# Selective scan in three clipped adds a step, with one group's decay on GpSimd, y copies on ScalarE and B's tables loaded ready-made

## What is computed

```python
xr, gate = jnp.split(x @ W_in.T, 2, axis=-1)
xc = jax.nn.silu(conv4(xr + t_emb))                  # depthwise, 4 taps
xn = layer_norm(xc) * ln_g + ln_b
Bm, Cm, dt = jnp.split(xn @ W_xproj.T, 3, axis=-1)
Ad = 1.0 + jnp.tanh(dt @ W_dt.T + b_dt) * 0.01 * A
Bd = Bm * jnp.minimum(norm(xn), 1.0)

def step(h, inputs):                                 # 64 steps, one after the other
    ad, bd, xt, ct = inputs
    h = jnp.clip(h * ad[:, :, None] + bd[:, :, None] * xt[:, None, :], -10.0, 10.0)
    yt = jnp.einsum('bd,bdh->bh', ct, h)
    return (h, yt)
...
return (y + D * xn) * jax.nn.silu(gate) @ W_out.T
```

## Time and profile before

| | us |
|---|---|
| median of 3 runs | 1787.09 (1785.98 to 1788.56) |
| the profiled execution, its own time | 1789.41 |
| its span, first to last instruction | 1787.6 |
| layer 2, pass 0, three written-out blocks (24 steps) | 80.8 |
| layer 3, the same | 80.4 |
| layer 3, the other 104 steps of the scan | 264.4 |
| one rolled block of eight steps | 20.3 |

### The profile page before, as it was taken

One profiled execution on the slowest core, in us unless ns is written; L12 is line 12 of the kernel. 1 busy time (PEld: TensorE's weight loads), 2 busy tenths in 40 slices (PEclk: granted clock), 3 DMA queues, 4 the chain that ended last, 5 costly groups with the idle time before them and its releaser, 6 DMA issues. The chain is left out here.

```text
span 1787.6 us, 42368 instructions
## 1 busy us (share of the span) xinstructions
PE 1637.6 (92%) x13764; PEld 703.0 (39%) x13764; DVE 1613.1 (90%) x2452; ACT 1296.5 (73%) x2197; POOL 621.5 (35%) x576
## 2 busy tenths in 40 slices
PE   7999999999999999888888889999997888888898
PEld 3555555555554455322111114444452221111144
DVE  5899999999986999889999998679998899999985
ACT  5655556455546999889999993069998899999920
POOL 0223233232331221365655560002223566555500
PEclk9999999999999999799999999999997999999999
DMA  4000000000001335544555666724445545556668
GB/s 162 2 1 0 1 2 32 2 1 0 1 1 72 139 149 177 191 163 132 182 160 188 219 189 202 239 83 157 144 159 185 179 132 183 155 189 196 189 223 288
DMA packets 126445, 226.56 MB, mean 127 GB/s; under 512 B 35617, under 2 KB 61217, under 8 KB 117537
## 3 DMA queue, kind: packets, MB, share of 16 engines
q1 hardware_dynamic: 125904, 223.30, 38.1%
q10 hardware_dynamic: 432, 1.84, 0.3%
HBM read 141.73 MB, written 83.36 MB: 126 GB/s over the span
## 5 line engine op out<-in xcount | busy, mean ns | idle before, releaser
L1038 ACT ACTIVATE R<-q,Ast 128x512 f32<-128x512 f32 x1008 | 627.0, 709 | 20.3 <-DVE q L2018 15.3
L2018 DVE CUSTOM_DVE_ANT_0 q<-R,PS 128x512 f32<-128x512 f32 x1008 | 617.3, 771 | 15.9 <-ACT R L1038 14.4
L1479 PE MATMUL PS<-xq,Uw 96*128 96x512 bf16 x1024 | 350.0, 396 | 82.3 <-DVE q L2018 71.4
L613 POOL TENSOR_TENSOR Uw<-Ub,rowmask 96x512 bf16<-96x512 bf16 x256 | 335.5, 1346 | 252.1 <-PE PS L1479 252.1
L1492 PE MATMUL PS<-q,Wy 128*32 128x512 f32 x2048 | 284.5, 618 | 0.3
L1479 PEld LDWEIGHTS PS<-xq,Uw 96*128 96x128 bf16 x1024 | 85.6, 97 | 471.1 <-DVE q L2018 399.3
L1152 PE MATMUL PS<-X,Win 128*128 (+1 forms) x456 | 214.5, 607 | 0.1
L1053 PE MATMUL PS<-xn,Wl 128*128 128x512 f32 x384 | 186.5, 609 | 0.8 <-DVE xn L1605 0.7
L1723 DVE SCALAR_TENSOR_TENSOR acc<-xp,Wc,acc 128x512 f32<-128x512 f32 x192 | 134.7, 752 | 2.6
L547 POOL TENSOR_TENSOR ex<-ex,rs 128x1024 f32<-128x1024 f32 x32 | 76.8, 2400 | 164.2 <-DVE rs L1628 164.2
L1152 PEld LDWEIGHTS PS<-X,Win 128*128 128x128 f32 x456 | 82.5, 191 | 92.5 <-issue 91.7
(11 more groups left out here) (159 smaller groups left out, 2491.9 us busy)
## 6 DMA issues: line engine op xcount, KB each, us to landing
xq<-xpart_d SPq DMA_DIRECT2D x384, 192.0 KB
sg_d<-sg SPq DMA_DIRECT2D x16, 1024.0 KB, 5.1
xn_d<-z SPq DMA_DIRECT2D x16, 1024.0 KB, 3.9
y_d<-ys SPq DMA_DIRECT2D x64, 256.0 KB, 3.9
xnp<-xn_d SPq DMA_DIRECT2D x16, 1024.0 KB, 8.4
sgp<-sg_d SPq DMA_DIRECT2D x16, 1024.0 KB, 11.5
xpart_d<-xh SPq DMA_DIRECT2D x16, 512.0 KB, 2.9
xpart_d<-xmi SPq DMA_DIRECT2D x16, 512.0 KB, 3.8
```

The source lines that it names most:

```text
L613: pl.tensor_tensor(Uw[0:XROWS, h, w, :, :, :], Ub[0:XROWS, w, 0:N, ds(s0, CH)].rearrange("p n t -> p t n").unsqueeze(2).broadcast_to([XROW ...
L1038: act.activation(R[:, w, :], q[:, (t + 1) % 2, w, :], ACT.Copy, scale=Ast[:, h, w, t:t + 1]).then_inc(ac_r, 1)
L1479: pe.matmul(PS[:, w, :], Uw[0:XROWS, h, w, t, :, :].rearrange("p b n -> p (b n)"), xq[0:XROWS, hb, w, s8 % XT, :], start=True, stop=True). ...
L2018: v._custom_dve(bass.dve_ops.TENSOR_ADD_SAT, out=q[:, s8 % 2, w, :], in0=R[:, w, :], in1=PS[:, w, :], s0=CLIP, s1=-CLIP).then_inc(dv_q, 1)
```

## The change

- **Three adds a step.** DVE's `step` adds columns 0 to 767 (group 0 and half of group 1), 768 to 1535 (the other half and group 2) and 1536 to 2047 (group 3), in this order; I call them add 0, add 1 and add 2. The four PSUM banks and the four tiles of `R` and `q` lie side by side, so one instruction runs across them. Add 0 waits for the matmuls of groups 0 and 1, add 1 for that of group 2, add 2 for that of group 3.
- **Group 1's decay on POOL** (`half_decay`), in two halves of 256 columns, with the counter `pd_r` ("decayed_odd_ready"). ACT keeps groups 0, 2 and 3; `ac_r` is now called "decayed_even_ready".
- **y copies** (`keep_y`) go from DVE to ACT.
- **B's tables.** B is turned on PE in the front (`turn_b`), split on DVE from PSUM and stored by `store_b` in pieces of 16 values into `bdiag_d`, an array in HBM that was filled with zeros once. `load_x` then reads finished block-diagonal weights `Uw`, 72 rows, with one more DMA for two steps. POOL's `Uw` instructions, the tables `Ub`, their clearing, `rowmask` and the rows of ones go away; `xq` and `Uw` have 72 rows in place of 96.
- The conversion `xmi` of the last group goes from POOL to ACT, and its `xlo` is done in halves between POOL's decays.

```diff
-                    for w in range(QW):
-                        v.wait_ge(pe_w, pi * (QW * S) + n * QW + w + 1 + W0)
-                        if w % 2 == 0:
-                            v.wait_ge(pe_yq, pi * (2 * S) + n * 2 - 4 + w // 2 + 1 + USED)
+                    for p, (begin, end, groups) in enumerate(((0, SPLIT, 2), (SPLIT, 2 * SPLIT, 3), (2 * SPLIT, QW * DI, QW))):
+                        state = q[:, s8 % 2, :, :].rearrange("p w c -> p (w c)")[:, begin:end]
+                        fed = PS[:, 0:QW, :].rearrange("p w c -> p (w c)")[:, begin:end]
+                        v.wait_ge(pe_w, pi * (QW * S) + n * QW + groups + W0)
+                        if p < 2:
+                            v.wait_ge(pe_yq, pi * (2 * S) + n * 2 - 4 + p + 1 + USED)
...
-                        v.wait_ge(ac_r, pi * RS + n * QW - QW + w + 1 + READY)
+                        if p < 2:
+                            v.wait_ge(pd_r, pi * (2 * (S - 1)) + n * 2 - 2 + p + 1 + READY)
+                        v.wait_ge(ac_r, pi * (3 * (S - 1)) + n * 3 - 3 + p + 1 + READY)
                         alone(v)
-                        v._custom_dve(bass.dve_ops.TENSOR_ADD_SAT, out=q[:, s8 % 2, w, :], in0=R[:, w, :], in1=PS[:, w, :],
+                        v._custom_dve(bass.dve_ops.TENSOR_ADD_SAT, out=state, in0=R[:, :, :].rearrange("p w c -> p (w c)")[:, begin:end], in1=fed,
                                       s0=CLIP, s1=-CLIP).then_inc(dv_q, 1)
...
                     for w in range(QW):
-                        if t == 0:
-                            pe.wait_ge(pl_u, cn * QW + w + 1)
-                        pe.wait_ge(dv_q, pi * (QW * S) + n * QW + w + 1)
-                        pe.matmul(PS[:, w, :], Uw[0:XROWS, h, w, t, :, :].rearrange("p b n -> p (b n)"),
+                        pe.wait_ge(dv_q, pi * (UN * S) + n * UN + (1, 2, 2, 3)[w])
+                        pe.matmul(PS[:, w, :], Uw[0:XROWS, hb, s8 % XT, w, :, :].rearrange("p b n -> p (b n)"),
                                   xq[0:XROWS, hb, w, s8 % XT, :], start=True, stop=True).then_inc(pe_w, 1)
...
+                def half_decay(pi, c2, s8, p):
+                    h, t = s8 // CH, s8 % CH
+                    if t < 2 and p == 0:
+                        pl.wait_ge(pl_a, pi * CHUNKS + c2 * 2 + h + 1)
+                    pl.wait_ge(dv_q, pi * (UN * S) + c2 * (8 * UN) + UN * s8 + p + 1)
+                    alone(pl)
+                    cols = slice(p * (DI // 2), (p + 1) * (DI // 2))
+                    pl.tensor_tensor(R[:, 1, cols], q[:, (t + 1) % 2, 1, cols], Ast[:, h, 1, t:t + 1].broadcast_to([P, DI // 2]),
+                                     ALU.mult).then_inc(pd_r, 1)
...
-                            for w in range(QW):
-                                act.wait_ge(dv_q, cn * (QW * CH) + QW * t + w + 1)
+                            for p, w in enumerate((0, 2, 3)):
+                                act.wait_ge(dv_q, cn * (UN * CH) + UN * t + p + 1)
                                 act.activation(R[:, w, :], q[:, (t + 1) % 2, w, :], ACT.Copy,
                                                scale=Ast[:, h, w, t:t + 1]).then_inc(ac_r, 1)
+                            if t == 1 and h == 0 and before:
+                                keep_y(pi, c2 * 2 - 1, 1)
...
+                def turn_b(it, dst):
+                    pe.wait_ge(rB_r, it + 1)
+                    pe.transpose(dst, rB[:, :], ident[:, :]).then_inc(bt_mm, 1)
...
+                pe.wait_ge(tv_s, (l * G + G - 2) * 4 + 2 + TV0)
                 for m in range(DC):
                     variance(l * G + G - 1, m, 6)
...
                 def load_x(ps, k):
+                    rows = bdiag_d[ps, 0:GB * DIAG].rearrange("(r f) -> r f", f=S * ROW)
+                    sp.dma_start(Uw[0:XROWS, k % XB, :, :, :, :].rearrange("p t w b n -> p (t w b n)"),
+                                 rows[:, k * (XT * ROW):(k + 1) * (XT * ROW)].unsqueeze(0)
+                                 .broadcast_to([PARTS, GB * PARTS, XT * ROW])).then_inc(xq_in[k % XB], 16)
```

More of the change, by code:

```diff
@@ L184, in cond_resid_kernel @@
         late = ExitStack()
+        sb("table_gap", [P, TT * DI + P], where=late)
         pass_tables.append(tables(1, late))
@@ L316, in _ @@
             sp.dma_start(fold[:, :], fold_d).then_inc(ld_late, 16)
-            sp.dma_start(rowmask[:, :], rowmask_d).then_inc(ld_late, 16)
             sp.wait_ge(w_mm, G * 2)
+            sp.wait_ge(zero_r, 1)
+            for ps in range(PASSES):
+                rest = bdiag_d[ps, 0:GB * DIAG].rearrange("(p k c) -> p k c", p=P, c=1024)
+                for k in range(GB * DIAG // (P * 1024)):
+                    sp.dma_start(rest[:, k, :], words(zeros).bitcast(bf16)).then_inc(zero_in, 16)
             def load_front(n):
@@ new lines, in last_half, with last_group @@
+                def last_half(it, k, b):
+                    if b == 0:
+                        pl.wait_ge(xmi_r, it * TT + k + 1)
+                        alone(pl)
+                    cols = slice(b * (DI // 2), (b + 1) * (DI // 2))
+                    low = pl.tensor_tensor(xlo[:, k, cols], xr1[:, k, cols], xmi[:, k, cols], ALU.subtract)
+                    if b:
+                        low.then_inc(xlo_r, 1)
+                def last_group(n):
+                    it = l * G + G - 1
+                    if n == 20:
+                        pl.wait_ge(xq_st, it * 48 + 48)
+                        alone(pl)
+                    if 20 <= n < 20 + 2 * TT:
+                        last_half(it, (n - 20) // 2, n % 2)
@@ new lines, in eight @@
+                def eight(ps, c2, first=False, last=False, tail=False):
+                    pi = l * PASSES + ps
+                    for s8 in range(8):
+                        for p in range(2):
+                            if not (first and s8 == 0):
+                                half_decay(pi, c2, s8, p)
+                        if tail:
+                            last_group(c2 * 8 + s8)
+                        if s8 == 0:
+                            if not first:
+                                stage_decay(ps, c2, 1)
+                        elif s8 == 1:
+                            if not first:
+                                stage_outputs(ps, c2, 1)
+                        elif s8 == 4 and not last:
+                            stage_decay(ps, c2 + 1, 0)
+                        elif s8 == 5 and not last:
+                            stage_outputs(ps, c2 + 1, 0)
+                        elif s8 == 5 and ps + 1 < PASSES:
+                            pl.wait_ge(tab_in[1], l * (16 * TABLES) + 16 * TABLES)
+                            alone(pl)
+                            stage_decay(ps + 1, 0, 0, True)
+                            stage_outputs(ps + 1, 0, 0)
+                        elif s8 == 7 and last and ps + 1 < PASSES:
+                            stage_decay(ps + 1, 0, 1, True)
+                            stage_outputs(ps + 1, 0, 1)
@@ L1025, in last_group, with last_middle, keep_y, decayed @@
                         high_part(it, 3, 7)
-                def decayed(pi, c2, first, between=None):
+                def last_middle(n):
+                    for k, at in enumerate((19, 21, 22, 23)):
+                        if n == at:
+                            middle_part(l * G + G - 1, k)
+                def keep_y(pi, ck, h):
+                    act.wait_ge(pe_yq, pi * (2 * S) + ck * (2 * CH) + 2 * CH + USED)
+                    act.wait_ge(y_out[h], pi * (CHUNKS // 2 * 16) + (ck - h) * 8 + 16)
+                    alone(act)
+                    act.activation(ys[:, h, :], PS[:, 4 + h, :], ACT.Copy).then_inc(ac_y, 1)
+                def decayed(pi, c2, first, before, between=None, after=None):
                     for h in range(2):
@@ L1340, in project_part @@
                 def project_part(it, part, done=None):
+                    if part == 2:
+                        pe.wait_ge(tv_s, it * 4 + TV0)
                     for m in range(DC):
@@ L2030, in eight @@
                         step(pi, c2, s8, first)
-                        if s8 == 1 and before:
-                            keep_y(pi, c2 * 2 - 1, 1)
-                        if s8 == 5:
-                            keep_y(pi, c2 * 2, 0)
                 for ps in range(PASSES):
@@ L2039, in _ @@
                     for c2 in range(plain):
-                        eight(pi, c2, c2 == 0, ps > 0 or c2 > 0, last_group if ps == 0 else None)
+                        eight(pi, c2, c2 == 0, last_group if ps == 0 else None)
                     with v.Fori(plain, CHUNKS // 2) as c2:
-                        eight(pi, c2, False, True)
-                keep_y(l * PASSES + PASSES - 1, CHUNKS - 1, 1)
+                        eight(pi, c2, False)
                 def gated(g):
```

254 lines of the change are left out of this document (98 added, 156 removed).

## The result

| | before | after |
|---|---|---|
| median, us | 1787.8 (1786.0 to 1789.7) | 1903.7 (1887.5 to 1909.6) |
| ratio | 1 | 1.063 (95%: 1.057 to 1.070) |
| profiled execution, its own time | 1789.4 | 1909.6 |
| its span | 1787.6 | 1907.8 |
| mean granted clock of TensorE | 0.983 | 0.924 |

The change makes the kernel 116 us slower. I had forecast slower, by 32 us.

What follows compares the result with a forecast made beforehand. The scan was taken as bound by DVE's columns and starts. Against 1789.4 us, rolled blocks +36, pass 1's written-out blocks -1, pass 0's -4 and start +1 gave 1821, as a median 1819 us; range 1766 to 1842.

Steps and rivals of the forecast that it cites:

- The adds and the new wait: Rolled scan blocks: DVE's work falls to 2.33 us a step, but 0.40 standstill before add 0 makes it 2.73, +1.5 a block.
- the sum: Whole kernel: all terms added to the profiled 1789.4 us, +32, 1821; as a median 1819 us.
- Who releases add 0: Rolled blocks: each DVE gap of about 0.4 us before add 0 is ended by PE's input matmul, never by POOL.
- The short wait as a rival: Rolled blocks: waits behind the matmul's are worked off while it is open, 2.47 us a step, 1770 us; chance 0.12.
- Written-out blocks of pass 0: Written-out scan blocks of pass 0: 67.5 + 5 + 2.2 + 4 = 78.7 us, -2 a layer, between -8 and +6.
- Pass 1's written-out block: Written-out blocks of pass 1: 0.14 us standstill, 2.47 a step; the two blocks together -1 us.
- Start: Front before the scan: PE waits for two instructions of B's split, short when read from PSUM; +0.5 us a layer.
- POOL: Scan: a half decay of 256 columns takes 0.67 us on POOL, two 1.3 a step, and never releases DVE.
- my limit: Rolled blocks after the change: ACT was to be busy under 80%.
- What lies beside this, at no cost: Scan work of ACT, PE, POOL and DMA, said to cost nothing; B's weights cost only SP's extra issue, 0.6 us or somewhat more.
- the rivals: Whole kernel: short wait everywhere, 1770 us (0.12); DVE stays full, 1737 (0.06); POOL is the bound, about 1853 (0.08).

Runs made afterwards that it cites:

- e1: The changed kernel, but after the first four buffers each load of Uw moves one row instead of 72; 1823.6 us, ratio 1.017.
- e4: e1 with DVE's wait for the input matmul moved from first to last of an add's waits; 1771.3 us.
- f1: The changed kernel with the 72 rows of Uw and x reordered, so B's load counts 24 rows outermost and 3 copies inside; 1828.3 us, ratio 1.022.

## Why the prediction was right, and where it was wrong

- **The adds and the new wait: right.** 0.40 us of standstill, 2.73 a step, 21.8 a block. e1 took 1823.6 us where the sum gave 1819. ACT was busy 2.17 us a step where I had 2.0, which cost nothing.
- **Who releases add 0: right,** though the rows of after name POOL. e4 shows it. The short wait as a rival (1770) does not hold in the changed kernel; with that wait moved last one gets its 2.45 a step, and 1771.
- **Written-out blocks of pass 0: right in layer 2.** From the first add to the first rolled step they take 78.8 us instead of 80.8 in layer 2, -2.0 as forecast, and 79.8 instead of 80.4 in layer 3, -0.6. The terms fit too: DVE busy 66.8 (67.5 in the sum), waits for ACT 4.1 (5), for PE 5.6 (6.2). Pass 1's written-out block became 0.3 us shorter, against a forecast of 0.5.
- **Start: right.** The first add comes at 744.47 instead of 743.88, +0.6 against +0.5. The four instructions of B's split take 0.28, 0.29, 0.38 and 1.14; the read from PSUM is a short one, as I had it.
- **POOL: right,** 0.61 instead of 0.67 a half, and no bound. ACT 80% in a rolled block, at my limit.
- **The step that failed** is the sentence in "What lies beside this, at no cost" that lets B's weights come "8 steps ahead by DMA" and costs only SP's issue. It put the transfer at nothing and priced the issue alone. It measured +84 us: 41 in layer 2, 43 in layer 3, in waits of PE for x and in steps of 3.68 at the low clock. That the forecast had the sign right says nothing for it: the 32 us forecast came from the new wait, and the larger part of the 116 from this term. What I should have weighed stood in two places. The rows gave 0.46 of DMA share in a rolled block, a mean over 16 engines, which looks like room for 144 KB; and the diff gave an access pattern with three copies outermost. The page of the Trainium skill that says what follows from it I had not set beside the diff.
- **The range** (1766 to 1842) therefore held e1 and f1, which are the change without that fault, and missed the change itself. None of the rivals was a late transfer, though the change moves work from an engine to DMAs, where that is the first to ask about.

## What to carry to other kernels

A DMA that replaces an engine's work is to be costed on the engines that carry it: count the outermost numbers of both sides, add up the fullest of the 16, and divide by the time of the step; a mean DMA share hides three full ones. If an instruction spans what two others free (here a PSUM bank), its loop is as long as the later of them, and the standstill can cost more than the instructions saved; giving the halves a bank each brought it back. And in a rolled loop the wait that ends last belongs last before its instruction: that alone was worth 52 us here.

## What the runs showed of the hardware

- In a rolled loop each wait that stands behind the late one adds about 0.09 us between event and add: 0.46 with three more against 0.18 with none (2.73 and 2.45 a step).
- The number of landings of a DMA goes with its outermost counts: 13 for 24 rows, 4 for three copies outermost; 52 a load, instead of 43, after the order was turned, and 75 us less. The same 144 KB a load added to the kernel before cost nothing with 13 landings and 25 us with 4.
- After a stop of PE for x of 5.29 us the granted clock was 0.50 in the trace's window behind it; a step is then 3.68 us and PE the bound.
- With input matmuls over 48 rows the clock stayed at 0.50 for 375 us at a PE that was busy throughout, in a program that took 2051.8 us. Over 96 rows, half of them with zero weights, and on another chip, it was 1.00 in every rolled block and the program, otherwise the same, took 1757.8 us. But one execution of the kernel before, with 96 rows, had a mean clock of 0.746 too. How the chip decides this no run here shows.
